# A mixture-of-experts layer on Trainium2: VectorE makes both low halves of the expert weights, GpSimd only scatters

## The reference, cut to what matters

```python
x = hidden_states.reshape(-1, 256)                          # here 2048 tokens
probs = softmax(x @ gate_w.T)                               # 64 experts
topk_w, topk_idx = top_k(probs, 6); topk_w /= sum(topk_w)
h = silu(einsum('th,eih->tei', x, experts_w1))              # 176 inner channels
y = einsum('tei,ehi->teh', h, experts_w2)                   # back to 256
out = sum of y over the 6 experts, weighted by topk_w
out += (silu(g) * u) @ shared_down.T                        # shared expert, g, u = x @ shared_gate_up.T
```

## Time and profile before

| | us |
|---|---|
| three timed runs | 1868.09, 1873.75, 1883.21 (median 1873.75) |
| the profiled execution | 1885.33 |
| its span in the profile | 1883.4 |

### The profile page before, as it was taken

How to read it: one execution, slowest core, us unless ns; L and a number is a source line. 1 busy time by engine, 2 the same in 40 slices (tenths; PEclk the granted TensorE clock), 3 DMA queues, 4 the chain that set the end, 5 groups by cost and what they waited for, 6 DMA issues and landing times. The chain is left out here.

```text
span 1883.4 us, 33921 instructions
## 1 busy us (share of the span) xinstructions
PE 1558.3 (83%) x9484; PEld 1165.7 (62%) x9484; DVE 1331.7 (71%) x2125; ACT 922.6 (49%) x1696; POOL 911.4 (48%) x714
## 2 busy tenths in 40 slices
PE   6689998699996899986999978716299999999931
PEld 5466665566664666654666648404198888878820
DVE  3568887588886688875888855503567777777767
ACT  3465554555554655546555533101076666666610
POOL 0334433434343444334344410566378999989920
PEclk8799999999998999998999985757599999999965
DMA  4012221022220112210221200334388888888744
GB/s 141 0 43 63 62 67 34 8 64 61 67 58 9 42 59 67 67 33 0 67 67 58 61 3 1 138 117 157 96 252 250 246 245 248 247 241 234 209 165 161
DMA packets 111029, 198.16 MB, mean 105 GB/s; under 512 B 17481, under 2 KB 63063, under 8 KB 110816
## 3 DMA queue, kind: packets, MB, share of 16 engines
q1 hardware_dynamic: 98656, 171.75, 30.9%
q0 software_dynamic: 12288, 25.41, 3.7%
HBM read 160.96 MB, written 44.50 MB: 109 GB/s over the span
## 5 line engine op out<-in xcount | busy, mean ns | idle before, releaser
L1307 POOL TENSOR_TENSOR ssq<-ssq,ysq 128x512 f32<-128x512 f32 x128 | 164.4, 1284 | 460.9 <-ACT ysq L759 460.9
L963 DVE SCALAR_TENSOR_TENSOR e<-bank,scal,e 128x511 f32<-128x511 f32 (+2 forms) x384 | 287.5, 749 | 54.3 <-ACT e L754 18.9
L1358 POOL DMA_INDIRECT outputs<-hsw,x_rows x160 | 243.1, 1519 | 33.3 <-issue 28.5
L461 PE MATMUL bank<-e,wn 128*128 128x512 f32 x512 | 252.8, 617 | 0.0
L386 PE MATMUL bank<-h_hi,wi_hi 128*128 x512 | 237.2, 463 | 18.8 <-POOL wi_lo L1294 14.6
L388 PE MATMUL bank<-h_hi,wi_lo 128*128 x512 | 204.9, 400 | 0.0
L387 PE MATMUL bank<-h_lo,wi_hi 128*128 x512 | 202.2, 395 | 0.0
L875 DVE TENSOR_TENSOR hid_lo_rows<-hid_rows,hid_hi_rows 88x256 fp32r<-88x256 f32 x160 | 120.9, 756 | 113.6 <-ACT hid_hi_rows L705 111.3
L754 ACT ACTIVATE e<-bank,scal 128x512 f32<-128x512 f32 x128 | 99.7, 779 | 199.0 <-PE bank L388 199.0
L1294 POOL TENSOR_TENSOR wi_lo<-wi,wi_hi 128x512 fp32r<-128x512 f32 x128 | 165.5, 1293 | 52.7 <-ACT wi_hi L705 52.7
L386 PE MATMUL bank<-hw_hi,ew_hi 128*88 128x128 f32 x640 | 161.0, 256 | 22.3 <-POOL ew_lo L1294 5.9
(11 more groups left out here) (245 smaller groups left out, 3764.3 us busy)
## 6 DMA issues: line engine op xcount, KB each, us to landing
ew<-expert_w SPq DMA_DIRECT2D x160, 432.0 KB
wi<-in_w SPq DMA_DIRECT2D x128, 256.0 KB, 2.7
x_rows<-grouped SPq DMA_DIRECT2D x160, 130.0 KB
wo<-out_w SPq DMA_DIRECT2D x128, 128.0 KB, 2.4
got<-outputs SPq DMA_DIRECT2D x16, 768.0 KB, 4.3
grouped<-zeros_out SPq DMA_DIRECT2D x65, 130.0 KB
outputs<-hsw,x_rows POOLq DMA_INDIRECT x160
x_all<-x_t SPq DMA_DIRECT2D x4, 512.0 KB, 8.6
```

What stands on the lines that cost most here:

```text
L461: i = mm(p_out[k][:, :], wn[:, par, k * P:(k + 1) * P], y[:, par, :], start=do_out == "first", stop=do_out == "last")
L963: v.scalar_tensor_tensor(dst[:, d:], src[:, 0:SEQ - d], taps(TAPS - 1 - d), dst[:, d:], ALU.mult, ALU.add).then_inc(S[done], 1)
L1307: g_.tensor_tensor(ssq[:, :], ssq[:, :], ysq[:, :], ALU.add).then_inc(S["ssq_done"], 1)
L1358: g_.indirect_dma_start(outputs, bass.IndirectOffsetOnAxis(x_rows[:, i % XD, EMB:EMB + 1].bitcast(U32), 0), y_rows[:, i % YD, :], None, bo ...
```

## The change

VectorE makes the low half of all 864 weight columns (`weights_low`), at the place where `second_weights` stood; `first_weights` goes from GpSimd, whose loop is now `scatter(i)` alone, directly behind `row_done(i)`. `w2_lo` and its waits go, and `first(i)` waits for `w_lo`, as before. The weights are two DRAM arrays and two transfers on one semaphore (so ScalarE waits for 32), W2 with its 88 rows unpadded; VectorE zeroes partitions 64 to 127 of the W2 columns of `ew` once, after the sends and behind the chain of shares, and SyncE waits for that (`zeros_set` 3) before its first load. SyncE reads four entries of a table at once (`four`). `fill(2)` becomes `fill(1)`.

```diff
@@ SyncE
-            def load_weights(i):
-                e = sp.value_load(owner_no[0:1, i:i + 1], min_val=0, max_val=EXPERTS - 1)
+            def load_weights(i, e):
                 sp.wait_ge(S["w_lo"], START["w_lo"] + i - 3)
-                sp.wait_ge(S["w2_lo"], START["w2_lo"] + i - 3)
-                sp.dma_start(ew[:, i % DEEP, :], expert_w[bass.ds(e, 1), :, :].rearrange("a p n -> p (a n)"))\
+                sp.dma_start(ew[:, i % DEEP, 0:W1_COLS], expert_w1[bass.ds(e, 1), :, :].rearrange("a p n -> p (a n)"))\
                     .then_inc(S[f"w_in{i % DEEP}"], 16)
+                sp.dma_start(ew[0:IHALF, i % DEEP, W1_COLS:ECOLS].rearrange("p (h n) -> p h n", h=2),
+                             expert_w2[bass.ds(e, 1), :, :, :].rearrange("a h p n -> p (a h) n"))\
+                    .then_inc(S[f"w_in{i % DEEP}"], 16)
+            def four(table, i, top):
+                return nc.values_load_multi_w_load_instructions(table[0:1, i:i + 4], engines=[mybir.EngineType.SP],
+                                                                min_val=0, max_val=top)[1]
...
+            sp.wait_ge(S["zeros_set"], 3)
+            early = four(first_row, 0, SPARE)
+            for i in range(DEEP):
+                load_rows(i, early[i])
+            owners = four(owner_no, 0, EXPERTS - 1)
+            for i in range(DEEP):
+                load_weights(i, owners[i])
+            for n in range(DEEP, ETILES, 4):
+                rows, owners = four(first_row, n, SPARE), four(owner_no, n, EXPERTS - 1)
+                load_rows(n, rows[0])
+                load_rows(n + 1, rows[1])
+                load_weights(n, owners[0])
+                load_rows(n + 2, rows[2])
+                load_weights(n + 1, owners[1])
+                load_rows(n + 3, rows[3])
+                load_weights(n + 2, owners[2])
+                load_weights(n + 3, owners[3])
@@ TensorE
             def second(i):
-                pe.wait_ge(S["w2_lo"], START["w2_lo"] + i + 1)
...
-                fill(2)
+                fill(1)
@@ ScalarE
             def weights(i):
-                act.wait_ge(S[f"w_in{i % DEEP}"], 16 * (i // DEEP + 1))
+                act.wait_ge(S[f"w_in{i % DEEP}"], 32 * (i // DEEP + 1))
@@ VectorE
-            def second_weights(i):
+            def weights_low(i):
                 dve.wait_ge(S["w_hi"], i + 1)
-                w = slice(W1_COLS, ECOLS)
-                low(ew_lo[:, i % DEEP, w], ew[:, i % DEEP, w], ew_hi[:, i % DEEP, w]).then_inc(S["w2_lo"], 1)
+                low(ew_lo[:, i % DEEP, :], ew[:, i % DEEP, :], ew_hi[:, i % DEEP, :]).then_inc(S["w_lo"], 1)
...
+            for q in range(HD):
+                dve.wait_ge(S[f"sent{q}"], 16 * TOP_K * GTILES // HD)
+            v.memset(ew[P // 2:P, :, W1_COLS:ECOLS], 0.0).then_inc(S["zeros_set"], 1)
+            weights_low(0)
             rows_in(0)
             rows_in(1)
-            second_weights(0)
             for i in range(ETILES):
                 if i + 2 < ETILES:
                     rows_in(i + 2)
                 dve.wait_ge(S["hid_hi"], i + 1)
                 low(hid_lo[0:IHALF, i % 2, :], hid[0:IHALF, i % 2, :], hid_hi[0:IHALF, i % 2, :]).then_inc(S["hid_lo"], 1)
                 if i + 1 < ETILES:
-                    second_weights(i + 1)
+                    weights_low(i + 1)
                 if i:
                     row_done(i - 1)
@@ GpSimd
             for i in range(ETILES):
-                first_weights(i)
-                if i >= 3:
-                    scatter(i - 3)
-            for i in range(ETILES - 3, ETILES):
                 scatter(i)
```

More of the change, by code:

```diff
@@ L76, in program @@
 def program(nc, x_t, in_w, out_w, scalars, bc_w, bc_conv, dt_w, dt_bias, a_log, c_t, mod_w, gate_w, shared_w,
-            shared_d, expert_w, const, route_const, grouped, outputs, out_t):
+            shared_d, expert_w1, expert_w2, const, route_const, grouped, outputs, out_t):
     ctx = ExitStack()
@@ L89, in program @@
                  "x_turned": 4, "x_lo": 2, "first_mm": 4, "second_mm": 4, "w_lo": 4, "hid_silu": 2, "hid_lo": 2,
-                 "row_done": 2, "w2_lo": 4, "acc_chain": 7, "acc_turned": 2, "final": 3}
+                 "row_done": 2, "acc_chain": 7, "acc_turned": 2, "final": 3}
         def sb(name, shape, dt=F32, on=ctx):
@@ L276, in program @@
             inner inner_silu prod weighted hw_hi hw_lo expert_mm result stored zero_set
-            w2_lo x_turned x_hi x_lo w_in0 w_in1 w_in2 w_in3 w_hi w_lo
+            x_turned x_hi x_lo w_in0 w_in1 w_in2 w_in3 w_hi w_lo
             first_mm hid_silu hid_hi hid_lo second_mm row_done
@@ L333, in _, with load_rows @@
                     load_out(b, PAIRS - 2 + par, par)
-            def load_weights(i):
-                e = sp.value_load(owner_no[0:1, i:i + 1], min_val=0, max_val=EXPERTS - 1)
+            def load_weights(i, e):
                 sp.wait_ge(S["w_lo"], START["w_lo"] + i - 3)
-                sp.wait_ge(S["w2_lo"], START["w2_lo"] + i - 3)
-                sp.dma_start(ew[:, i % DEEP, :], expert_w[bass.ds(e, 1), :, :].rearrange("a p n -> p (a n)"))\
+                sp.dma_start(ew[:, i % DEEP, 0:W1_COLS], expert_w1[bass.ds(e, 1), :, :].rearrange("a p n -> p (a n)"))\
                     .then_inc(S[f"w_in{i % DEEP}"], 16)
-            def load_rows(i):
-                row = sp.value_load(first_row[0:1, i:i + 1], min_val=0, max_val=SPARE)
+                sp.dma_start(ew[0:IHALF, i % DEEP, W1_COLS:ECOLS].rearrange("p (h n) -> p h n", h=2),
+                             expert_w2[bass.ds(e, 1), :, :, :].rearrange("a h p n -> p (a h) n"))\
+                    .then_inc(S[f"w_in{i % DEEP}"], 16)
+            def load_rows(i, row):
                 if i >= XD:
@@ L348, in load_rows @@
                 sp.dma_start(x_rows[:, i % XD, :], grouped_rows[bass.ds(row, P), :]).then_inc(x_in[i % XD], 16)
+            def four(table, i, top):
+                return nc.values_load_multi_w_load_instructions(table[0:1, i:i + 4], engines=[mybir.EngineType.SP],
+                                                                min_val=0, max_val=top)[1]
             sp.wait_ge(S["fill_rows"], 1)
-            for e in range(EXPERTS):
-                row = sp.value_load(fill_row[0:1, e:e + 1], min_val=0, max_val=SPARE - P)
-                sp.dma_start(grouped_rows[bass.ds(row, P), :], zeros_out[:, :]).then_inc(S["xs_zero"], 16)
+            for e in range(0, EXPERTS, 4):
+                for row in four(fill_row, e, SPARE - P):
+                    sp.dma_start(grouped_rows[bass.ds(row, P), :], zeros_out[:, :]).then_inc(S["xs_zero"], 16)
             sp.wait_ge(S["owners"], 2)
@@ L1348, in _ @@
                                           h_send[:, g % HD, k, :], None).then_inc(S[f"sent{g % HD}"], 16)
[L1350 to L1353, removed]
             def scatter(i):
@@ L1389 @@
     w1 = np.asarray(L0_ffn_experts_w1).reshape(EXPERTS, EXP_INNER, KE, P).transpose(0, 3, 2, 1).reshape(EXPERTS, P, -1)
-    w2 = np.asarray(L0_ffn_experts_w2).transpose(0, 2, 1).reshape(EXPERTS, 2, IHALF, EMB).transpose(0, 2, 1, 3)
-    w2 = np.pad(w2.reshape(EXPERTS, IHALF, -1), ((0, 0), (0, P - IHALF), (0, 0)))
+    w2 = np.asarray(L0_ffn_experts_w2).transpose(0, 2, 1).reshape(EXPERTS, 2, IHALF, EMB)
     down = np.zeros((SH_CHUNKS * P, EMB), np.float32)
@@ L1408 @@
         "shared_d": rows(down),
-        "expert_w": np.concatenate([w1, w2], 2),
+        "expert_w1": w1,
+        "expert_w2": w2,
         "const": constants(),
```

## The result

The changed kernel takes 2043.37 us (median of four runs, 2038.61 to 2081.04) against 1873.64 for the kernel before: a ratio of 1.088, 95% interval 1.083 to 1.094. Two more runs took 2033.64 and 2075.91. The ratio is that of the four of these six runs with a mean granted clock of 0.887 to 0.899 (2033.64 to 2043.82, mean 2039.75); the other two had 0.848 and 0.842. The prediction was 2031 us with a range of 2010 to 2115. The profiled execution is the slowest (2081.04, span 2079.3), and its excess over the others has a cause that the trace shows, TensorE's clock.

What follows compares the result with a forecast made beforehand. GpSimd was taken to bound the loop before, a closed ring through TensorE, ScalarE and VectorE after. 1885.33 profiled + 143 for the ring + 14 for the start = 2042, 2031 us on the median (11.6 lower); range 2010 to 2115.

Steps and rivals of the forecast that it cites:

- The ring: Expert-tile loop: first(i+1) waits through VectorE's weights' low half for tile i, so no overlap; 3.63 us a tile, +143 us.
- Hidden terms: Expert-tile loop: all other work, such as copies, rows, scatter and loads, fits into 3.63 us a tile.
- The loads: Weight transfers in the expert loop: 2.4 us a tile, bounds up to 0.3 less and 3.9, hidden under 3.63.
- the busiest DMA engine: Expert loop: W2's 88 rows would go to 11 of 16 engines, the busiest needing about 2.7 us, hidden.
- The start, +14 us: Start of the expert stage: serial zeroing and loads make first(0) 14 us later than 1365.47; bounds 8 and 20.
- The zero-fills by fours change nothing: Before the expert stage: reading the zero-fill table by fours gains nothing, since GpSimd's sends end later.
- the memset: Start of the expert stage: VectorE zeroes half the partitions of ew behind the chain of shares, 1.25 us, ending at 1366.0.
- rival A: Expert loop: TensorE's clock falls as well; +78 us, 2109 us, or 2188 if held down all the stage; chance 0.19.
- its own work lifts it: Argument against A: the loop began at the low clock and was at 1.00 from 1374 us on.
- the alternation: Expert loop under A: the clock goes up and down, about 4.1 us a tile, +78 us, 2109 us.
- Rival B: Expert loop: the ring doesn't close and GpSimd's relief decides; about 2.25 us a tile, -62 us, 1812 us; chance 0.05.
- Rival C: Expert loop: the transfers decide at their upper bound, 3.9 us a tile, +43 us, 2074 us; chance 0.06.

Runs made afterwards that it cites:

- Opening the ring: The changed kernel with weights_low(i+1) put ahead of VectorE's wait for hid_hi(i), nothing else different: 1843.18 us, ratio 0.983 to the kernel before.
- shortening one link by 0.53 us: The changed kernel with two unread products and the weights' low half in two instructions, first waiting for the W1 part alone: 1916.84 us, ratio 1.035.
- with two products: The changed kernel with two unread products a tile in place of one: 2029.03 us, ratio 1.083.
- the order with the weights first: The changed kernel with VectorE's weights_low(i+1) ahead of both rows_in(i+2) and the hidden tile's low half: 1808.86 us, ratio 0.976.
- The kernel with fours alone: The kernel before with only the table of its 64 zero-fills read by fours, loop untouched: 1870.27 us, ratio 0.996.
- the change with GpSimd's part back: The changed kernel with W1's low half back on GpSimd, VectorE at the W2 columns alone, two semaphores restored: 1875.93 us, ratio 1.002.

## Why the prediction was right

**The ring.** "3.63 us a tile": measured 3.62 wherever the clock is up, in the change and in four experiments. Its links were 1.25 + 0.48 + 0.45 + 0.34 + 1.05 + 0.06 in the prediction. In the rows above, high half to low half is 0.45 (1802.94 to 1803.39), low half to weights 0.34, the weights 1.05, the handoff 0.05. Opening the ring brought back 200 us, moving the low half alone reproduced the loss, undoing it removed the loss, and shortening one link by 0.53 us shortened the tile by 0.53. The mean with the clock up is a little more, 3.65: with two products every sixteenth tile took 3.90 us, for a cause that wasn't looked for, and a few early ones ran at the low clock.

**Hidden terms.** The scatter was to be near 1.0 and is 0.98 at the median. The loads were to hide at 2.4 us a tile, and a share of 0.56 at 3.62 is 2.0, so the smaller pieces cost nothing beside the ring and their price lay near the lower bound. The 2.7 us that the prediction worked out for the busiest DMA engine was too much: the order with the weights first has the same transfers and took 2.37 a tile in the mean. How many engines carry the 88 rows no run shows. `hid_lo` took 0.42, as said.

**The start, +14 us: wrong in sign.** `first(0)` came 4.7 us earlier. "The zero-fills by fours change nothing" is the step that failed: with them `first(0)` starts 15 us sooner in the traces of the kernel before and 25 in those of the changed one. The prediction also had the memset behind the chain of shares, where it stood behind the sends (5.57 us of waiting), and at 1.25 us where 64x2048 took 1.76. The kernel with fours alone (`first(0)` at 1350.26) and the change with GpSimd's part back (1353.63) have their first sends at the same time, 1192.56 and 1192.20, so their difference, about 3 us, is roughly what zeroing and later loads cost (other edits of the change are in it too), where the prediction had 14. The later sends of the changed kernel go with the other 7: 1365.47 - 15.2 + 3.4 + 7.1 = 1360.8.

**The clock, rival A: too low a chance.** I wrote "its own work lifts it" and gave A 0.19. It did fall, to some degree in every run of the change: about 11 us in the trace of a usual one, 52 in that of the profiled one (632.74 - 580.74). The price of a tile held down was near, 4.48 for 4.62, but the alternation was milder than the 78 us given.

**Luck in the number.** The predicted 2031 comes near by errors that cancel. Too high was the start, by some 19 us. Too low were the clock, taken as free (11), the loop without it (146.9 for 143), and the 11.6 us taken off for the median. The kernel before had started the stage late in its profiled execution, 15 us later than with the fours, and the 4.7 us are counted from that same start, so nothing more was to come off. 2031 - 18.7 + 10.6 + 3.9 + 11.6 = 2038, where the usual runs have 2039.75.

**Rival B** said that the ring of the changed kernel doesn't close. It closes. But its price for a loop without the ring, 1812 us or a ratio of 0.967, was near: the order with the weights first has 0.976. The prediction's other figure for B, 2.7 us a tile because VectorE's subtractions shut out the scatter, did not come: with the ring open the scatter did grow, to 1.56 and 1.20 us at the median, but a tile took 2.51 and 2.37. **Rival C** didn't decide at 3.62 us, and appears at 2.15.

## What to carry to other kernels

When work moves from an engine that is the bottleneck to one that has room, its place in the order of the new engine counts for more than its length. Here 0.37 us more on an engine busy 75% cost 0.9 us a tile, because it stood behind a wait on the tile before; ahead of that wait a tile took 0.22 us less than in the kernel before, and 0.36 less as VectorE's first work of all. And work that nobody reads can be what holds TensorE's clock: a change that removes it has to be timed with and without it.

## What was not expected of the hardware

**The scatter's length depends on what VectorE is doing when it starts.** In the changed kernel hardly a scatter overlaps VectorE's low halves, and all take 0.98 to 1.00 us. With the ring open they take 0.98 to 1.83. In the rows of the opened ring the scatter ends 0.86 us after VectorE's 128x864 subtraction both times (1700.16 to 1701.02, 1702.72 to 1703.58), though one started 0.35 us into it and the other 0.11; between 1400 and 1750 us that is so for 106 of the 108 scatters that start inside one. The two exceptions began 0.02 us after its start and 0.07 before its end, and took 0.98. None of the 30 that began 0.1 us or more before one was held. From the same kernel's timeline, the scatter:

```profile
1471.27 0.98 POOL L1368 DMA_INDIRECT outputs<-hsw,x_rows  x1 [0.91 <-DVE hsw L1264]
```

and the subtraction:

```profile
1471.82 1.05 DVE L888 TENSOR_TENSOR ew_lo<-ew,ew_hi 128x864 fp32r<-128x864 f32 x1
```

They overlap by 0.43 us and neither is longer. The Trainium skill (SBUF — State Buffer, "SBUF: two separate sides") says that a GpSimd instruction that reads SBUF and a VectorE one with two SBUF inputs exclude each other for the whole instruction, whichever starts first. The rows agree in one direction only: the scatter is held by a subtraction that runs when it starts, and a scatter under way holds nothing up. In the kernel before, the 1.60 us fit as well: one scatter started at 1501.21, inside VectorE's subtraction for the hidden tile (1500.53 to 1501.33), the 128x512 one followed without a gap (1501.26 to 1501.94), and the scatter ended 0.87 after that, at 1502.81.

**The clock ran at both levels under one program.** In one execution of the changed kernel, tiles of the same work ran at 0.50 from 1380 to 1500 us and at 1.00 from 1680 to 1900.
